# Linear attention's split weights stored in device memory after the first batch and read back for the other three; the values' low parts moved from VectorE to GpSimd

## What is computed

```
q = x @ Wq.T + bq;  k = x @ Wk.T + bk;  v = x @ Wv.T + bv      # x is the layer-normed input
sq, sk = elu(q) + 1, elu(k) + 1
kv = einsum('bhsd,bhse->bhde', sk, v)                           # 128 x 128 per head
qkv = einsum('bhsd,bhde->bhse', sq, kv)
norm = einsum('bhsd,bhd->bhs', sq, sk.sum(axis=2))
attn = qkv / (norm[..., None] + EPS)
out = x + attn.reshape(b, s, H * D) @ Wo.T
```

## Time and profile before

| | us |
|---|---|
| median of 3 runs (3746.47 to 3748.72) | 3746.49 |
| the profiled execution's own time | 3749.1 |
| its span, first to last instruction | 3747.4 |
| granted TensorE clock, mean | 0.98 |
| linear attention's query steps, in the trace | 122 to 799 |

### The profile page before, as it was taken

The page is one execution under the profiler, slowest core; times in us unless marked ns, Lnnn a source line. Parts: engine busy times, 40 slices in busy tenths (PEclk is TensorE's granted clock), DMA queues, the critical chain, the costliest instruction groups (busy, mean ns, idle before and its releaser), DMA issues.

```text
span 3747.4 us, 52800 instructions
## 1 busy us (share of the span) xinstructions
PE 3391.4 (90%) x19398; PEld 2853.6 (76%) x19398; DVE 2742.9 (73%) x5009; ACT 2060.3 (55%) x3891; POOL 1140.2 (30%) x1507
## 2 busy tenths in 40 slices
PE   2788888879999999999999999999999999999993
PEld 1677777767878888788887887878887888788872
DVE  4787897757786777776777677776777767776764
ACT  2567766745545555555555555555555555556541
POOL 2577877842212212122121221212212121122103
PEclk9999999989999999999999999999999999999996
DMA  2000001110000000000000001000000010000000
GB/s 75 20 24 24 25 28 35 43 32 12 15 14 27 21 13 12 12 21 26 12 13 13 23 19 40 12 12 24 26 14 13 18 29 25 12 23 22 25 6 28
DMA packets 81103, 83.27 MB, mean 22 GB/s; under 512 B 8272, under 2 KB 76496, under 8 KB 80720
## 3 DMA queue, kind: packets, MB, share of 16 engines
q1 hardware_dynamic: 80848, 79.89, 7.2%
HBM read 74.62 MB, written 5.24 MB: 21 GB/s over the span
## 4 chain that ended last, share of the span: by engine, by line
PE 64%; DVE 8%; ACT 5%; issue 1%; DMA 0%; POOL 0%; DVEq 0%; SPq 0%; ACTq 0%; POOLq 0%
PE at_ps_t L1717 12%; PE at_ps_job L35 6%; PE at_ps_job L37 6%; PE at_ps_job L36 6%; PE at_ps_o L37 5%; PE at_ps_o L35 5%; PE at_ps_o L36 5%; PE at_ps_s L37 5%; PE at_ps_s L35 5%; PE at_ps_s L36 5%; DVE at_probT_lo L1598 2%; ACT at_probT_hi L1544 1%; ACT x_resident L1587 1%; PE at_ps_job L852 1%; DVE ch_r L742 1%
## 5 line engine op out<-in xcount | busy, mean ns | idle before, releaser
L1544 ACT ACTIVATE at_probT_hi<-at_ps_t 128x512 fp32r<-128x512 f32 x1024 | 611.2, 597 | 1152.4 <-PE at_ps_t L1717 1152.2
L1598 DVE TENSOR_TENSOR at_probT_lo<-at_ps_t,at_probT_hi 128x512 fp32r<-128x512 f32 x1024 | 705.1, 689 | 377.1 <-ACT at_probT_hi L1544 365.4
L1717 PE MATMUL at_ps_t<-ident,x_resident 128*128 128x128 f32 x4096 | 625.6, 275 | 103.1 <-DVE at_probT_lo L1598 92.3
L1717 PEld LDWEIGHTS at_ps_t<-ident,x_resident 128*128 128x128 f32 x4096 | 481.0, 140 | 254.9 <-DVE at_probT_lo L1598 113.8
L1652 DVE TENSOR_REDUCE at_neg_max<-at_ps_s 128x1 f32<-128x1024 f32 x512 | 623.0, 1217 | 10.9 <-PE at_ps_s L37 2.4
L1587 ACT ACTIVATE x_resident<-at_ps_s,at_neg_max 128x1024 f32<-128x1024 f32 x512 | 569.4, 1112 | 12.9 <-DVE at_neg_max L1652 9.8
L1527 POOL TENSOR_TENSOR at_w_hi<-at_w_raw,ch_cols 128x256 fp32r<-128x256 f32 x192 | 117.7, 613 | 1196.5 <-PE at_ps_job L37 1175.4
L35 PE MATMUL at_ps_o<-at_probT_hi,at_v_lo 128*128 128x512 f32 x1024 | 445.8, 435 | 2.4 <-DVE at_oT_lo L1628 2.4
L35 PE MATMUL at_ps_s<-at_k_hi,at_q_lo 128*128 128x512 f32 x1024 | 447.3, 437 | 0.0
L37 PE MATMUL at_ps_s<-at_k_lo,at_q_hi 128*128 128x512 f32 x1024 | 405.3, 396 | 0.0
L37 PE MATMUL at_ps_o<-at_probT_lo,at_v_hi 128*128 128x512 f32 x1024 | 404.0, 395 | 0.0
(11 more groups left out here) (275 smaller groups left out, 7781.5 us busy)
## 6 DMA issues: line engine op xcount, KB each, us to landing
at_w_raw<-attn_w SPq DMA_DIRECT2D x256, 128.0 KB, 2.3
at_w_raw<-mlp_w SPq DMA_DIRECT2D x112, 128.0 KB, 2.3
li_wq_raw<-lin_q_w SPq DMA_DIRECT2D x64, 128.5 KB, 2.1
li_wo_raw<-lin_out_w SPq DMA_DIRECT2D x32, 256.0 KB, 3.0
x_resident<-x SPq DMA_DIRECT2D x4, 1024.0 KB, 10.8
out<-x_resident SPq DMA_DIRECT2D x4, 1024.0 KB, 5.0
li_raw<-mlp_w SPq DMA_DIRECT2D x16, 128.0 KB, 2.4
ch_r<-lin_kv_w SPq DMA_DIRECT2D x1, 1024.0 KB, 6.7
```

The costliest lines, as they stand in the source:

```text
L1544: nc.scalar.activation(ph[:, i // TC, 4 * half:4 * half + 4, (i % TC) * P:(i % TC + 1) * P], ps_t[:], ACT.Copy).then_inc(s_ph, 1)
L1598: nc.vector.tensor_tensor(pl[at], ps_t[:], ph[at].bitcast(F32), ALU.subtract).then_inc(s_pl, 1)
L1717: last = nc.tensor.transpose(ps_t[:, j, :], prob[:, i % 2, kt * P:(kt + 1) * P], sh.ident[:])
```

## The change

Four edits.

1. Query weights. In the first batch SyncE writes both parts of each split head to device memory (`keep_wq`). For the other 48 heads it reads them back straight into `li_wq_hi` and `li_wq_lo` (`fetch_wq`), and GpSimd splits nothing. The read of head hh waits on SyncE for q steps 0 to 2 * hh - 3, as it overwrites the buffer that they use.
2. Output weights likewise: `keep_wo` for the eight slices of the first batch, `fetch_wo` for the other 24, in place of a load, a rounding on ScalarE and a low part on GpSimd. A read overwrites the single pair `li_wo_hi`, `li_wo_lo`, so it waits for the MADE before.
3. The biases of all heads come in one load and are prepared once; the ScalarE and VectorE instructions read a column of them.
4. The low parts of keys and values are one GpSimd instruction of 512 columns; VectorE's L1259 goes.

The core of the diff:

```diff
+            def fetch_wq(hh):
+                if hh == H:
+                    sp.wait_ge(s_wq_kept[0], 32 * (H // 2))
+                    sp.wait_ge(s_wq_kept[1], 32 * (H // 2))
+                sp.wait_ge(s_q, 2 * hh - 2)
+                sp.dma_start(wqh[:, hh % 2, :].bitcast(F32), wq_kept[hh % H, 0]).then_inc(s_wq_back[hh % 2], 16)
+                sp.dma_start(wql[:, hh % 2, :].bitcast(F32), wq_kept[hh % H, 1]).then_inc(s_wq_back[hh % 2], 16)
...
+            def fetch_wo(i):
+                if i == 2 * KVH:
+                    sp.wait_ge(s_wo_kept, 32 * 2 * KVH)
+                sp.wait_ge(c.made, made("MADE", (i - 1) // 2, (i - 1) % 2))
+                sp.dma_start(woh[:].bitcast(F32), wo_kept[i % (2 * KVH), 0]).then_inc(s_wo_back, 16)
+                sp.dma_start(wol[:].bitcast(F32), wo_kept[i % (2 * KVH), 1]).then_inc(s_wo_back, 16)
...
             for t in range(BEGIN, plan.end):
-                if t % 2 == 0 and t >= 0 and t // 2 + 2 < B * H:
-                    load_wq(t // 2 + 2)
-                if t - 1 in made_time and wo < 2 * KVH * B:
-                    load_wo(wo)
-                    wo += 1
+                if t % 2 == 0 and 0 <= t < 2 * H:
+                    keep_wq(t // 2)
+                for hh in ((t // 2 + 2,) if t >= 0 and t % 2 == 0 else ()) + ((H,) if t == 2 * H - 2 else ()):
+                    if hh < H:
+                        load_wq(hh)
+                    elif t != 2 * H - 4 and hh < B * H:
+                        fetch_wq(hh)
+                if t - 1 in made_time:
+                    i = made_time[t - 1]
+                    if i < 2 * KVH:
+                        keep_wo(i)
+                    if i + 1 < 2 * KVH:
+                        load_wo(i + 1)
+                    elif i + 1 < 2 * KVH * B:
+                        fetch_wo(i + 1)
                 for part, v in mlp_pieces(c, t):
...
-                    nc.gpsimd.tensor_tensor(kvl[:, i, 0:PK], z[:, k % 3, 0:PK], kvh[:, i, 0:PK].bitcast(F32),
+                    nc.gpsimd.tensor_tensor(kvl[:, i, 0:2 * PK], z[:, k % 3, :], kvh[:, i, 0:2 * PK].bitcast(F32),
                                             ALU.subtract).then_inc(s_kl, 1)
-                if -2 <= t and t // 2 + 1 < B * H:
-                    (take_bias if t % 2 else split_wq)(t // 2 + 1)
-                if t + 1 in made_time:
+                if t % 2 == 0 and 0 <= t < 2 * H - 2:
+                    split_wq(t // 2 + 1)
+                if made_time.get(t + 1, 2 * KVH) < 2 * KVH:
...
-                if t - 3 in kv_time:
-                    k, v, i = kv_time[t - 3]
-                    dve.wait_ge(s_kvh, k + 1)
-                    nc.vector.tensor_tensor(kvl[:, i, PK:2 * PK], z[:, k % 3, PK:], kvh[:, i, PK:2 * PK].bitcast(F32),
-                                            ALU.subtract).then_inc(s_vl, 1)
```

More of the change, by code:

```diff
@@ L958, in linear_attention_phase @@
         woh, wol = pair("wo", [P, CH])
-        wq_raw = sb("wq_raw", [P, 2, KT * HD + 1], F32)
+        wq_raw = sb("wq_raw", [P, 2, KT * HD], F32)
         wqh, wql = pair("wq", [P, 2, KT * HD])
-        bias = sb("bias", [P, 2, 2], F32)
+        wq_kept = nc.dram_tensor("li_wq_kept", (H, 2, P, KT * HD), F32).ap()
+        wo_kept = nc.dram_tensor("li_wo_kept", (2 * KVH, 2, P, CH), F32).ap()
+        bias_in = sb("bias_in", [P, H], F32)
+        bias = sb("bias", [P, 2, H], F32)
         norm = sb("norm", [P, TC], F32)
@@ L973, in linear_attention_phase @@
         s_const, s_small, s_w, s_wh, s_wl, s_ones = (sem(n) for n in ("const", "small", "w", "wh", "wl", "ones"))
-        s_xs, s_ek, s_phik, s_kvh, s_kl, s_vl, s_kvs = (sem(n) for n in ("xs", "ek", "phik", "kvh", "kl", "vl", "kvs"))
+        s_xs, s_ek, s_phik, s_kvh, s_kl, s_kvs = (sem(n) for n in ("xs", "ek", "phik", "kvh", "kl", "kvs"))
         s_wo, s_woh, s_wol = (sem(n) for n in ("wo", "woh", "wol"))
         s_wq = [sem("wq0"), sem("wq1")]
-        s_wqh, s_wql, s_bias = (sem(n) for n in ("wqh", "wql", "bias"))
+        s_wqh, s_wql, s_bias_in, s_bias = (sem(n) for n in ("wqh", "wql", "bias_in", "bias"))
+        s_wq_kept, s_wq_back = ([sem(f"{n}{i}") for i in range(2)] for n in ("wq_kept", "wq_back"))
+        s_wo_kept, s_wo_back = sem("wo_kept"), sem("wo_back")
         s_q, s_uq, s_eq, s_f, s_ph, s_pl, s_y, s_norm, s_rn, s_x, s_y3, s_x3 = (sem(n) for n in (
@@ L1053, in split_wq @@
                     pool.wait_ge(s_q, 2 * hh - 2)
-                nc.gpsimd.tensor_tensor(wqh[:, par, :], wq_raw[:, par, 0:KT * HD], c.zero.to_broadcast([P, KT * HD]),
+                    pool.wait_ge(s_wq_kept[par], 32 * (hh // 2))
+                nc.gpsimd.tensor_tensor(wqh[:, par, :], wq_raw[:, par, :], c.zero.to_broadcast([P, KT * HD]),
                                         ALU.add).then_inc(s_wqh, 1)
                 pool.wait_ge(s_wqh, hh + 1)
-                nc.gpsimd.tensor_tensor(wql[:, par, :], wq_raw[:, par, 0:KT * HD], wqh[:, par, :].bitcast(F32),
+                nc.gpsimd.tensor_tensor(wql[:, par, :], wq_raw[:, par, :], wqh[:, par, :].bitcast(F32),
                                         ALU.subtract).then_inc(s_wql, 1)
[L1060 to L1066, removed]
+            pool.wait_ge(s_bias_in, 16)
+            nc.gpsimd.tensor_tensor(bias[:, 0, :], c.zero.to_broadcast([P, H]), bias_in[:], ALU.subtract).then_inc(s_bias, 1)
+            nc.gpsimd.tensor_tensor(bias[:, 1, :], bias_in[:], c.one.to_broadcast([P, H]), ALU.add).then_inc(s_bias, 1)
+            split_wq(0)
             for t in range(BEGIN, plan.end):
@@ L1133, in _ @@
                     act.wait_ge(s_q, t + 1)
[L1134 removed]
+                    act.wait_ge(s_bias, 2)
                     if t >= 2:
@@ L1293, in job @@
                     pe.wait_ge(c.taken, by_dve["TURN", v, 0])
-                    pe.wait_ge(s_wol, 2 * v + part + 1)
+                    i = 2 * v + part
+                    if i < 2 * KVH:
+                        pe.wait_ge(s_wol, i + 1)
+                    else:
+                        pe.wait_ge(s_wo_back, 32 * (i - 2 * KVH + 1))
                     last = split3(nc, out[:], kvTh[:, v % 2, :], kvTl[:, v % 2, :], woh[:], wol[:], start=True, stop=True)
@@ L1302, in _ @@
                 if q_step(t):
-                    if t % 2 == 0:
+                    if t % 2 == 0 and t // 2 < H:
                         pe.wait_ge(s_wql, t // 2 + 1)
+                    elif t % 2 == 0:
+                        pe.wait_ge(s_wq_back[t // 2 % 2], 32 * (t // 2 // 2 - H // 2 + 1))
                     if t >= 2:
```

27 lines of the change are left out of this document (17 added, 10 removed).

## The result

The changed kernel takes 3789.1 us (median of 4 runs, 3783.7 to 3790.2), the kernel before beside it 3747.6 (3746.5 to 3749.2). The ratio is 1.0107, with an interval of 1.0094 to 1.0119: slower by 1.1%. The forecast was 3754.5 in a range of 3728 to 3771. The direction was right; the size, five times too small, was not, and the time lies outside the stated range. The profiled execution's span is 3788.5 us, 41.1 more than before.

A forecast was written before the change was run, and what follows sets the result against it. No engine was taken as full throughout; the bound changes by stretch, VectorE full in the third and fourth. Costs +9 +6 +15 +6 = +36 against relief -28 gave net +8: 3746.5 + 8 = 3754.5 us, range 3728 to 3771.

The forecast's parts named there:

- the least length of the steps with the wait: MADE step pairs, batches 1 to 3: MADE 4.4 us after q's end, pair floor 12.35 us; +9 and +6 (sixth stretch).
- the low clock behind it: TensorE idle 2.9 us in MADE steps, then matmuls at 1.2 GHz, 1.6 us each time: +15 (bounds 0 and 22).
- the relief elsewhere: Less work and waiting on VectorE, GpSimd and ScalarE outside the stretches' floor: -13 -1 -5 -3 -3 -3 = -28 us.
- The stretches: Six runs of steps with MADE every other step (33 to 38 through 113 to 118): +9 +6 and clock +15.
- The subtraction of four spells: Four of the 18 MADE steps already had a low-clock spell, so only 14 x 0.8 x 1.6 = 18 us was charged.
- The 3 us taken off as hidden in VectorE's full stretches: Low-clock cost taken as partly hidden where VectorE is full, third and fourth stretches: 18 us lowered to 15.
- The late pieces: Routed layer's loads behind the gated pair: low part for step 94 some 5 us late, steps 96 and 109 about 1; +6.
- The 13 behind the stretches: Behind the first five MADE stretches, 20 of VectorE's L1259 go, 18.9 us, of which 13 counted as gain.
- The 3 for a quieter port: VectorE's other instructions blocked less on the port shared with a less busy GpSimd: -3 us.
- Relief whole and clock holding: Rival: VectorE's relief shows fully and TensorE's clock stays up; 3730 us, chance 0.27.
- Cancelling: Rival: trace's slack in MADE steps takes half of the wait; within 7 us of now, 3746 us, chance 0.25.
- GpSimd as the bound in the first batch: Rival: wider GpSimd instruction makes 16 first-batch tiles and 8 routed-layer splits 0.56 us later each; +13, 3768 us, chance 0.08.
- the signs named: Profile after: 18 of 24 MADEs wait for `li_wo_kept`, clock below 1, 1.3 us low part, sixth stretch about 30 us.

The follow-up runs named there:

- The filled run: Changed kernel with twelve further 512-column matmuls, overwritten by MADE, ahead of the wait for stored Wo in 18 MADEs; 3763.4 us, ratio 1.0039.
- the low part alone: Kernel before with only GpSimd making the whole 512-column low part of keys and values, VectorE's 64 instructions removed; 3734.6 us, ratio 0.9964.
- the good order: Changed kernel with SyncE issuing Wo's pair and the routed layer's pieces ahead of the query weights' pair; 3707.7 us, ratio 0.9892.
- Wo's pair first: Changed kernel with SyncE issuing only the pair for Wo ahead of the pair for the query weights; 3721.2 us, ratio 0.9929.

## Why the prediction was wrong in size

It named the place, the cause and the 18 steps. The mechanism was right; three terms of the sum were mis-sized: the least length of the steps with the wait (+15 for +23), the low clock behind it (+15 for +24.5), and the relief elsewhere (-28 for about -14). Against the spans, +41.1 instead of +8:

**The stretches: predicted +9 +6 +15 = +30, measured +47.6.** The filled run splits it. The *floor* at full clock was sound where it was worked out step by step: predicted 12.35 us a pair, 38.22 / 3 = 12.7 measured in steps 81 to 86; for the sixth stretch 9.9 predicted, 32.76 / 3 = 10.9 measured. Over all six it is +23.1 (230.0 - 206.9) for +15: q's end to MADE took 4.7 us, not 4.4, which is 5 of the 8 us between, and in the fifth stretch, whose jobs I only guessed at, 41.2 us stand against 39.4. The *clock* is 24.5 us for 15. One spell costs what I said (24.5 / 16 = 1.5 us), but it came in 16 of 18, not in 0.8 of 14. The subtraction of four spells was a fault of reasoning in part: where the floor, built at full clock, takes the place of an old length, the old spell has gone with it and must not be taken off again. It fits where an old length was kept, as in the third stretch, which holds two of the four. The 3 us taken off as hidden in VectorE's full stretches were another fault: the third and the fourth lost 3.5 and 3.6 us to the clock (42.75 - 39.22 and 41.86 - 38.22). In the fourth VectorE, busy 29.9 of 41.9 us, no longer set the length.

**The late pieces: +6, measured +7.5** as changed, step 94 being 10.5 us long for 3.7. Right, though it is 13.9 once Wo's pair is early: step 98 then takes 11.0 us, where it takes 5.8 in the changed kernel, between two MADE waits.

**The relief: -28, of which about -14 shows.** Outside the stretches the kernel is 6.5 us shorter, the pieces' loss included. The first batch gave 5.4 (165.5 us for 170.8), as said, and the low part alone gives 5.0 of it. The rest, 22 by prediction, is some 9. The 13 behind the stretches was the term with the least under it: the low part alone, on the kernel before, makes the steps between and behind the stretches some 6 us shorter. The 3 for a quieter port came to nothing: VectorE's other instructions take 422.0 us for 422.5 (above), because the wide instruction takes back what the stored weights give. And steps 103 to 112 lost 4.4 us, which the sum didn't have. About 2 of these are step 110, where TensorE stands 1.8 to 2.2 us before a job on `ch_r_rounded` in all ten kernels that store the query weights, and in neither of the two that don't. Why stays open.

**What the whole change is worth.** In the good order it gains 41 us: 13.5 by the low part (16 if it is added last), some 4.5 by the query weights and bias, which the noise doesn't tell from nothing, and 22.5 by Wo. The order takes 81 away: 67 by Wo's pair, of these about 25 by the clock, and 14 by the pieces. The prediction had the relief in the stretches only as far as it would shorten them below the floor, which is right for the changed kernel, and so never asked what the change would give without its order.

**The rivals.** Relief whole and clock holding (3730): neither held. Of the 43 us of relief some 14 show in the changed kernel, and the clock fell; with the clock held by the fill the time is still 3763. With 3.5 us from q's end to MADE, near the 3.3 from which it was to decide, the time was 3758. Cancelling (3746): no. MADE starts 3.35 us later behind q with the wait (4.71 in the filled kernel, 1.36 with Wo's pair first), 60 us over 18 steps, of which 38.9 show in the stretches. So slack takes a third and not half, and the clock comes on top. GpSimd as the bound in the first batch: no, the first batch is 7 us shorter with the wide instruction than without. Its second half, the steps of the routed layer's splits, is borne out: in the good order steps 103 to 112 take 49.9 us with the wide instruction and 46.6 without. Of the signs named, the 18 waits, the exception of the six first MADEs, the clock below 1 and the 1.3 us on GpSimd came true, and of the six stretches behind the MADEs three are 2 to 5 us shorter. The sixth stretch is 40.5 us instead of about 30.

## What to carry to other kernels

A load stands behind every wait that is ahead of it on its queue: list, for each transfer, the latest event that any earlier entry of the queue waits for, and put the loads in the order in which these events come. Here two blocks of a loop in the other order are worth 81 us of 3789 and turn a loss of 1.1% into a gain of 1.1%. When TensorE is to stand still for some 3 us in a step that it bounds, charge the low clock behind nearly every such wait: here 13 to 17 of 18, at some 1.5 us each.

## What the runs showed of the hardware that was not expected

- Matmuls whose result is overwritten, put into a wait of TensorE, gave back 25.5 us of 3789: 12 a step, 18 steps. The wait kept its length, 4.7 us from q's end, and the granted clock went from 0.75 to 0.96 in the stretches to 1.00 in all six.
- The clock does not fall at a sharp length of wait. It fell behind 16 of 18 waits of 3.2 us on average (17 and 13 in two other kernels with the same waits), and behind 10 of 18 of 2.0 us. Of four waits of 2.05 us in one kernel it fell behind three.
- Four transfers issued within 1.4 us (768 KB in all), in the same order: at step 81 the second slice of Wo landed 3.0 us from its issue in one kernel and 4.6 in another.
- A GpSimd instruction of 512 columns in place of one of 256 raised the median of one VectorE instruction beside it from 445 to 631 ns, in the kernel before with only the low part moved.
- The Trainium skill, DMA: Bandwidth & Descriptors, Rules for kernel authors, says to issue early and wait late because the fixed cost then overlaps. The trace agrees, and here it is the whole transfer that overlaps: it takes 3 us, and the 67 us of the order are 3.7 for each of the 18 MADEs.
